# Mamba-2 block and mixture of experts on one core: late steps of a tile put in another order, another way into the experts, and five down products per experts' tile in place of six

## What is computed

```python
# block: y of the state-space layer, 1024 inner channels, 16 heads of 64, state 128
zxbcdt = u @ in_proj_w.T                    # z, xBC, dt
xBC = silu(conv_b + causal 4-tap conv of xBC)
y = Y_diag + Y_off + x * D_skip             # decays from cumsum(dt * A), states carried on
y = y * silu(z); y = y * rsqrt(mean(y*y) + EPS) * norm_w
o = y @ out_proj_w.T
# experts: 8 experts, hidden width F = 192, top 2 per token
gate, up = x @ w_gate_proj[e].T, x @ w_up_proj[e].T
out = sum_e weight[e] * ((silu(gate) * up) @ w_down_proj[e].T)
```

## Time and profile before

| what | us |
|---|---|
| median of 3 runs | 699.69 |
| the profiled execution | 697.2 |
| its span in the profile | 695.2 |
| TensorE busy | 637.0 (92%) |
| VectorE busy | 507.8 (73%) |
| ScalarE busy | 373.6 (54%) |
| GpSimd busy | 294.0 (42%) |
| DMA, mean over the span | 116 GB/s |

### The profile page before, as it was taken

One profiled execution on the slowest core, in us unless ns is written; L12 is line 12 of the kernel. 1 busy time (PEld: TensorE's weight loads), 2 busy tenths in 40 slices (PEclk: granted clock), 3 DMA queues, 4 the chain that ended last, 5 costly groups with the idle time before them and its releaser, 6 DMA issues.

```text
span 695.2 us, 12667 instructions
## 1 busy us (share of the span) xinstructions
PE 637.0 (92%) x4215; PEld 522.4 (75%) x4216; DVE 507.8 (73%) x1098; ACT 373.6 (54%) x787; POOL 294.0 (42%) x209
## 2 busy tenths in 40 slices
PE   4998899999999999989999989898988899999991
PEld 3896687868879678776877967665677788899981
DVE  6998868877977887787797698999786644444430
ACT  4778936564654754557376373638245444444431
POOL 2011344526435454453544424341136665656641
PEclk9999999999999999999999999998999999999996
DMA  8672014305113131530412304083594766767663
GB/s 269 231 288 92 1 39 145 122 11 173 60 64 122 62 123 32 151 123 1 152 51 103 96 28 130 1 272 115 172 305 80 132 123 117 125 120 123 125 100 45
DMA packets 31890, 80.38 MB, mean 116 GB/s; under 512 B 4768, under 2 KB 10016, under 8 KB 29664
## 3 DMA queue, kind: packets, MB, share of 16 engines
q1 hardware_dynamic: 22784, 58.23, 25.4%
q0 software_dynamic: 9056, 21.50, 17.1%
HBM read 59.93 MB, written 19.79 MB: 115 GB/s over the span
## 4 chain that ended last, share of the span: by engine, by line
PE 61%; DVE 17%; issue 7%; DMA 7%; ACT 5%; POOL 2%; SPq 0%; DVEq 0%; ACTq 0%; POOLq 0%
PE pi L1471 17%; PE po L1510 11%; PE pg L1685 9%; PE pd L1698 7%; DVE xs L959 5%; PE py L1566 3%; PE py L1573 3%; PE px L1668 2%; DMA out<-yo,idx 2%; DVE y L1244 2%; PE pxb L1557 2%; PE pxb L1588 2%; ACT m L675 1%; DMA m<-cs_d 1%; DMA out<-o 1%
## 5 line engine op out<-in xcount | busy, mean ns | idle before, releaser
L1471 PE MATMUL pi<-xh,whl 128*128 128x256 f32 x1152 | 165.1, 286 | 1.8 <-DVE zs L965 1.3
L1471 PEld LDWEIGHTS pi<-xh,whl 128*128 128x128 f32 x1152 | 146.3, 188 | 4.6 <-issue 2.4
L959 DVE SCALAR_TENSOR_TENSOR xs<-raw,conv_w,xs 128x256 f32<-128x256 f32 x240 | 112.1, 532 | 11.0 <-ACT xs L650 10.9
L1510 PE MATMUL po<-wo,y 128*128 128x512 f32 x256 | 114.8, 602 | 0.5 <-DVE y L1256 0.5
L1471 PE MATMUL pi<-xl,whl 128*128 128x256 f32 x576 | 91.7, 281 | 0.0
L1510 PEld LDWEIGHTS po<-wo,y 128*128 128x128 f32 x256 | 48.1, 193 | 55.4 <-issue 55.2
L551 POOL DMA_INDIRECT out<-yo,idx x39 | 62.0, 1590 | 61.2 <-ACT yo L817 32.4
L675 ACT ACTIVATE m<-m,cs_tok 128x128 f32<-128x128 f32 x256 | 79.7, 389 | 0.5
L1471 PEld LDWEIGHTS pi<-xl,whl 128*128 128x128 f32 x576 | 78.4, 188 | 0.0
L1685 PE MATMUL pg<-ew,xgh 128*128 x312 | 64.6, 349 | 0.0
L524 POOL TENSOR_TENSOR carry<-carry,cd 128x1024 f32<-128x1024 f32 x14 | 27.8, 1987 | 79.6 <-PE py L1566 79.6
(11 more groups left out here) (220 smaller groups left out, 1161.9 us busy)
## 6 DMA issues: line engine op xcount, KB each, us to landing
m<-cs_d SPq DMA_DIRECT2D x16, 1024.0 KB, 6.5
e<-cs_d SPq DMA_DIRECT2D x30, 256.0 KB, 4.6
ew<-in_w_gu SPq DMA_DIRECT2D x8, 768.0 KB, 9.5
w_as_read<-in_w_in SPq DMA_DIRECT2D x9, 512.0 KB, 8.3
res<-in_x SPq DMA_DIRECT2D x16, 256.0 KB, 2.8
out<-o SPq DMA_DIRECT2D x16, 256.0 KB, 2.0
xin<-in_x SPq DMA_DIRECT2D x6, 512.0 KB, 3.6
xn_d<-xin SPq DMA_DIRECT2D x6, 512.0 KB, 2.8
```

Of the source, the lines that this page charges most:

```text
L959: dve.scalar_tensor_tensor(out=xs[par][:, b, :], in0=raw[:, b, k:k + GT], scalar=conv_w[:, b, k:k + 1], in1=xs[par][:, b, :], op0=ALU.mult ...
L1471: mm = pe.matmul(bank[:, hf, :], whl[:, weight(g, n), lo, k, hf * P:(hf + 1) * P], xx[:, k, :], start=k3 == 0, stop=k3 == 11)
L1510: mm = pe.matmul(po[:, :], y[:, b, :], wo[:, b, :], start=b == 0, stop=b == XB - 1)
```

## The change

It does four things.

1. **Even tiles 2 to 12.** VectorE does `finish(t - 1)` after `own(1)` and `carried()`, no longer before them. SyncE's store of that output and load of the next residual go into the odd tile after, behind `load_decays2`.
2. **Tiles 13 to 15.** `probabilities` goes behind `carried()` in tile 13; `experts_of_tiles` goes to tile 15, in two parts (4 and 7 instructions). ScalarE's high halves of expert 0 go behind the `btok` copy of tile 15.
3. **The seam.** Two more buffers take the gathered rows of slot tiles 2 and 3, so these wait for the end of `own` in tile 15 and not for the turning of tiles 0 and 1. GpSimd waits for `factor(15)` before gathers 4 and 5, and then itself stores the last tile's output once `finish(15)` is done. SyncE no longer does.
4. **Five down products.** `h` is 256 channels wide: channels 0 to 127, then 128 to 191 twice (two instructions on VectorE). The down weights' second block holds channels 128 to 191 twice too, with the high half of the weights in partitions 0 to 63 and the low rest in 64 to 127. So one product gives high x (high + low) of the rest. The weights of an expert take 128 partitions where they took 96; `down_low` is two instructions.

```diff
-ph = [phs[0:FH, i, :, :] for i in range(2)]
+ph = [phs[:, i, :, :] for i in range(2)]
...
+xg_more = [Area(nc, second + i * D * 4, zs_at)(f"xg{2 + i}", [P, D]) for i in range(2)]
+hh = [es(f"hh{i}", [P, 2, P], F32R) for i in range(2)]
+hl = [es(f"hl{i}", [P, 2, P], F32R) for i in range(2)]
...
                 if t > 1 and c == 1:
                     load_decays2(t)
+                    if t < T - 2:
+                        store(t - 2)
+                        load_res(t - 1)
...
-                if t:
+                if t and (c == 1 or t == T - 2):
                     store(t - 1)
                     load_res(t)
...
-            store(T - 1)
-            sp.wait_ge(o_out, 16 * T)
+            sp.wait_ge(o_out, 16 * (T - 1))
...
             def gather(j):
-                if j >= 2:
+                to, arrived = (xg_more, xg_more_in) if j in (2, 3) else (xg, xg_in)
+                if j in (2, 3):
+                    pool.wait_ge(yd, 2 * T)
+                elif j in (4, 5):
+                    pool.wait_ge(gtr, j - 3 + CR)
+                elif j > 5:
                     pool.wait_ge(gtr, j - 1 + CR)
...
-            for j in range(4):
+            for j in range(6):
                 gather(j)
-            factor(T - 1)
+                if j == 3:
+                    factor(T - 1)
+            pool.wait_ge(o_done, T)
+            pool.dma_start(out_t[T - 1], o[:, :]).then_inc(last_out, 16)
             for j in range(1, J + 2):
-                if j + 3 < J:
+                if 2 < j < J - 3:
                     gather(j + 3)
...
-                    gate_up_high(act, 1)
-                    down_high(act, 1)
+                    for e in range(2):
+                        gate_up_high(act, e)
+                        down_high(act, e)
...
-            dve.tensor_tensor(d_lo(e), d_lo(e).bitcast(F32), d_hi(e).bitcast(F32), ALU.subtract).then_inc(d_lo_done, 1)
+            dve.tensor_tensor(d_lo(e)[:, 0:D], d_lo(e)[:, 0:D].bitcast(F32), d_hi(e)[:, 0:D].bitcast(F32), ALU.subtract)
+            dve.tensor_tensor(d_hi(e)[FR:P, D:2 * D], d_lo(e)[FR:P, D:2 * D].bitcast(F32),
+                              d_hi(e)[FR:P, D:2 * D].bitcast(F32), ALU.subtract).then_inc(d_lo_done, 1)
...
                 if t == T - 1:
+                    experts_of_tiles(0)
                     variance(t - 1)
                     decayed(0)
                     finish(t - 1)
+                    experts_of_tiles(1)
                     table()
...
-                if t == T - 3:
-                    probabilities()
...
-                if 0 < t < T - 1:
+                if 0 < t < T - 1 and (c == 1 or t == T - 2):
                     finish(t - 1)
...
                 if 0 < t < T - 2:
                     carried()
+                    if c == 0:
+                        finish(t - 1)
                 if t == T - 3:
-                    experts_of_tiles()
+                    probabilities()
...
-                dve.tensor_tensor(h[:, :], hg[:, :], pg[par][:, F:2 * F], ALU.mult).then_inc(h_done, 1)
+                dve.tensor_tensor(h[:, 0:F], hg[:, :], pg[par][:, F:2 * F], ALU.mult)
+                dve.tensor_tensor(h[:, F:2 * P], hg[:, P:F], pg[par][:, F + P:2 * F], ALU.mult).then_inc(h_done, 1)
...
-                for xx, ww in ((hh, dh), (hh, dl), (hl, dh)):
-                    for k in range(2):
-                        mm = pe.matmul(pd[par][:, :], xx[par][:, k, :], of(ww, e, k), start=n == 0, stop=n == 5)
-                        n += 1
+                pe.matmul(pd[par][:, :], hh[par][:, 0, :], of(dh, e, 0), start=True, stop=False)
+                pe.matmul(pd[par][:, :], hh[par][:, 0, :], of(dl, e, 0), start=False, stop=False)
+                pe.matmul(pd[par][:, :], hh[par][:, 1, :], of(dh, e, 1), start=False, stop=False)
+                pe.matmul(pd[par][:, :], hl[par][:, 0, :], of(dh, e, 0), start=False, stop=False)
+                pe.matmul(pd[par][:, :], hl[par][0:FR, 1, :], of(rest, e, 1), start=False, stop=True).then_inc(down, 1)
```

More of the change, by code:

```diff
@@ L28 @@
 E, F = 8, 192
-FH = F // 2
+FR = F - P
 T = TOKENS // P
@@ L1150, in table, with experts_of_tiles @@
                 dve.tensor_tensor(prob[:, :], prob[:, :], given(5), ALU.add).then_inc(prob_done, 1)
-            def experts_of_tiles():
+            def experts_of_tiles(part):
                 by_step = ef[:, :].rearrange("o (i two) -> o two i", two=2)
                 low, high = slice(0, (J - 3) // 2), slice(1, (J - 1) // 2)
-                dve.wait_ge(tab_in_s, 16)
                 route.after()
[L1157 to L1160, removed]
-                route.after()
-                route.step(dve.tensor_scalar(ef[:, 0:J], ef[:, 0:J], float(E - 1), None, ALU.min))
-                route.after()
-                dve.tensor_copy(eidx[:, :], ef[:, 0:J]).then_inc(eidx_done, 1)
+                if part == 0:
+                    route.step(dve.tensor_tensor(ecmp[:, :, :], tabc[0:1, TAB["tile"]].unsqueeze(2).broadcast_to([1, J, E]),
+                                                 end[0:1, :].unsqueeze(1).broadcast_to([1, J, E]), ALU.is_ge))
+                    route.after()
+                    route.step(dve.tensor_reduce(ef[:, 0:J], ecmp[:, :, :], AX.X, ALU.add))
+                    route.after()
+                    route.step(dve.tensor_scalar(ef[:, 0:J], ef[:, 0:J], float(E - 1), None, ALU.min))
+                    route.after()
+                    dve.tensor_copy(eidx[:, :], ef[:, 0:J]).then_inc(eidx_done, 1)
+                    return
+                route.step(dve.tensor_tensor(ecmp[:, 1:J, 0], ef[:, 1:J], ef[:, 0:J - 1], ALU.is_gt))
                 route.step(dve.scalar_tensor_tensor(out=pf[:, :], in0=by_step[:, 1, high], scalar=float(E),
@@ L1167, in experts_of_tiles @@
                 route.after()
+                route.step(dve.scalar_tensor_tensor(out=ecmp[:, 1:J, 1], in0=ecmp[:, 1:J, 0], scalar=16.0,
+                                                    in1=tabc[0:1, TAB["lag"]][:, 1:J], op0=ALU.mult, op1=ALU.add))
                 route.step(dve.scalar_tensor_tensor(out=pf[:, :], in0=pf[:, :], scalar=float(E),
@@ L1174, in experts_of_tiles @@
                 dve.tensor_copy(packed[:, :], pf[:, :]).then_inc(eidx_done, 1)
-                route.step(dve.tensor_tensor(ecmp[:, 1:J, 0], ef[:, 1:J], ef[:, 0:J - 1], ALU.is_gt))
-                route.after()
-                dve.wait_ge(ctap, 3 * CB * G)
-                route.step(dve.scalar_tensor_tensor(out=ecmp[:, 1:J, 1], in0=ecmp[:, 1:J, 0], scalar=16.0,
-                                                    in1=tabc[0:1, TAB["lag"]][:, 1:J], op0=ALU.mult, op1=ALU.add))
-                route.after()
-                dve.tensor_copy(landed[:, 1:J], ecmp[:, 1:J, 1]).then_inc(eidx_done, 1)
             statistics(0)
@@ L1663, in turn @@
             def turn(j, par, r):
-                pe.wait_ge(xg_in[par], r * 16 + 16)
+                rows = xg[par]
+                if static(j, 2, 3):
+                    pe.wait_ge(xg_more_in[par], 16)
+                    rows = xg_more[par]
+                elif static(j, 0, 1):
+                    pe.wait_ge(xg_in[par], 16)
+                else:
+                    pe.wait_ge(xg_in[par], r * 16)
                 if not static(j, 0):
@@ L1782 @@
     gu = np.concatenate([a["L0_ffn_w_gate_proj"], a["L0_ffn_w_up_proj"]], axis=1)
+    down = a["L0_ffn_w_down_proj"].transpose(0, 2, 1)
     arrays = {
```

34 lines of the change are left out of this document (15 added, 19 removed).

## The result

| | before | after |
|---|---|---|
| median, us | 699.41 (695.89 to 702.23, 10 runs) | 693.64 (689.95 to 694.61, 10 runs) |
| profiled execution, us | 697.2 | 692.66 |
| span, us | 695.2 | 690.9 |

The ratio is 0.9924 [0.9897, 0.9951]: faster by 5.8 us, where 15.4 were forecast. In the after kernel the lines are: turning of the next tile L1607, `carried` L1280, `off` L1585, `diag` L1592, projection L1529, turning of x L1694, gate and up L1711, the five down products L1721 to L1725, turning of h L1733, `h` in two pieces L1398 and L1399.

The account below looks back on a forecast made before the run. TensorE was taken to bound the kernel, nearly full in scan and experts. Terms 4.0 + 5.5 + 5.5 + 0.4 = 15.4 us took the profiled 697.2 to 681.8; plus 2.5 for the median, 684.3 us, range 678.5 to 691.5.

Parts of the forecast that it names:

- part 1: Even scan tiles: moving finish behind carried takes 0.66 us off each of six stalls, 4.0 us; ends 0 and 6.1.
- parts 2 and 3: Tiles 13 to 15 and first slot tiles: 2.6 + 4.1 - 1.2 for the clock, 5.5 us; ends 0 and 9.
- part 3: First slot tiles: timely gathers and an earlier store bring hidden tile 0 to 8 from 42.3 to 38.2, 4.1 us gained.
- part 4 with the tail: Experts: five down products save 0.19 us in each of 29 steps, 5.5 us, plus 0.4 behind the last gate product.
- The forecast's own sign of being wrong: Experts: a step of 4.1 us or more, where 3.98 us between down products was expected.
- The room in the loop through h: Experts: slack before TensorE must wait for h, put at 0.30 us in one tile and 0.39 in the next.
- the loop through h takes it all: Experts: second h instruction at full 0.23 us plus 0.15 more leaves five down products gaining 0; 690.2 us, chance 0.12.
- an h held up by GpSimd: Experts: second h instruction waits for GpSimd in each of 29 tiles; at 0.6 us longer, 707.2 us; chance 0.03.
- Part 2: Tiles 13 to 15: waits for own(0) and btok go; last projection starts 2.6 us sooner, before 1.2 off for the clock.
- the loss by the clock: Before the last projection: idle TensorE drops its clock, costing 1.5 to 2.7 us; with late gathers 689.8 us, chance 0.10.

Follow-up runs that it names:

- part 1 alone: Kernel before, with only finish moved behind carried in even tiles 2 to 12, with its store and residual load: 694.92 us, ratio 0.9932.
- parts 1 to 3: Changed kernel with the six down products of before, 96 channels each, and h in one instruction: 690.20 us, ratio 0.9877.
- parts 1 and 2: Kernel before with the moved finish and the new order in tiles 13 to 15, gathers and last store as before: 689.88 us, ratio 0.9892.
- the full product: Changed kernel with the fifth down product over all 128 rows, where it took 64: 688.99 us, ratio 0.9853.
- the order with the gate products first: Changed kernel, fifth product over 128 rows, gate products ahead of down products from slot tile 9: 692.28 us; with four gathered-row buffers too, 684.51 us.
- the three kernels with the extra products: Unread products added in tile 15: nine or four to the changed kernel with 128-row fifth product (690.62, 688.56 us); four with gate-first order, four buffers (683.24 us).

## Why the prediction was wrong

| term | forecast | measured, and from which kernels |
|---|---|---|
| part 1 | 4.0 | 3.9 (before, part 1 alone) |
| parts 2 and 3 | 5.5 | 4.7 (part 1 alone, parts 1 to 3) |
| of which part 3 | 4.1 | -0.3 (parts 1 and 2, parts 1 to 3) |
| part 4 with the tail | 5.9 | -3.4 (parts 1 to 3, after) |
| sum | 15.4 | 5.2 |

The terms are differences of medians from different rounds, so they add up to 5.2 and not to the 5.8 of the result. By the ratios to the kernel before in the same rounds, with intervals estimated from theirs, part 1 is 4.7 +- 1.6 us, parts 2 and 3 are 3.8 +- 3.1, part 3 is 1.0 +- 3.6 and part 4 is -3.3 +- 3.2. The sign of part 4 rests on the steps in the traces as well; the split between parts 2 and 3 is weak.

**Part 4 is the step that failed**, and in it the sentence "The fifth has 64 rows, but a product's time goes by its columns, which stay". The product itself is no slower, since the second of two neighbours takes 0.24 us; the two changes of rows cost 0.19 + 0.15 = 0.34 us a step, and 0.233 is what the sixth product had cost: +0.11, with 29 steps 3.1 us. The steps themselves took 2.5 us more than before (124.16 for 121.67). The forecast's own sign of being wrong, a step of 4.1 or more, is there. No row I showed of before had an operand of 64 rows between two of 128, so the cost needed bounds from both sides, and I gave it none. The Trainium skill has a rule that speaks to it and that I had not weighed: TensorEngine Tiling (Array Packing), Key Properties, says: "Changing tiling mode (not just tile) drains the TensorE". It stands under a list with modes of 32 and 64 rows. The slots of 0.42 and 0.43 us agree with it, but the skill gives no price, and nothing here asked for a mode, only for an operand of 64 rows; that the mode changed is not shown.

**The room in the loop through h** was the second mistake of the same part, hidden until the first was mended: with the full product the mean step is 4.194 for 4.196, a gain of nothing. So the rival "the loop through h takes it all" had the mechanism, at a chance of 0.12, and nearly the time: 690.2 us, against 688.99 with the full product. What I mis-sized is "When TensorE really waits for h, it is 0.26". That row is of an early tile, in which TensorE had been idle for 0.81 us. It is 0.29 again in slot tile 1 of the full-row kernel, but 0.45 and 0.55 in its steady steps, where TensorE is still busy with the down products when h comes; whether that is the reason is not shown. Against the 0.56 of the earlier trace rows that leaves 0 to 0.1 of room, not 0.30 to 0.39. The second h instruction then costs 0.48 - 0.35 = 0.13 (628.88 less 628.40, less one h), and taking it out gave 0.12 a step. That the loop is the bound is shown by the order with the gate products first: 3.93 us, 0.24 less than before, the 0.233 of the sixth product. With both bounds out of the way the medians go from 690.20 (parts 1 to 3) to 684.51, 5.7 us, near the 5.9 that I had for part 4 alone. The other rival of this part, an h held up by GpSimd, did not come: the second h instruction takes 0.21 us.

**Part 2 was probably undersized, and of its rival the loss by the clock came true.** The projection began 7.1 us sooner, against 6.6 forecast, and lost 1.43 by the clock, where I had 1.2. Alone, part 2 is worth 694.92 - 689.88 = 5.0 us by the medians and 2.8 by the ratios, where I had 2.6 - 1.2 = 1.4. The clock's cause, TensorE's idle time in tile 15, is shown: in the three kernels with the extra products the projection takes 7.1 us, in all the others with part 2 it takes 8.0 to 8.8. TensorE was ready for tile 15 sooner than I had shifted it (the projection in that tile begins 8.6 us sooner, 471.19 for 479.77, where I had 6.3), and VectorE, which I had bounding that tile, gave the start of the last one. That parts 2 and 3 together come near their 5.5 is luck, as far as the split can be trusted: one gave more than its term and the other nothing.

**Part 3** rested on rows 6: gathers late and the first add late. The gathers were hardly late any more: in these tiles the profile shows no wait of a product for rows, where it had four, 2.8 us. The add was, by 5.63 us: on GpSimd's queue the store is issued at 508.11, when `o` is ready, and the add can go only 6.2 us later. The wait for it had been 6.47 from SyncE's queue, so the new queue took little off. Of the 41.0 us, 1.6 are the slots of part 4 (39.4 with full rows) and 1.7 the store (37.7 without it), which leaves 37.7, near the 38.2 of the forecast. What remains are the waits for h, 6.9 us at the turning's weight loads with full rows, with the weights' rests on VectorE, which I had counted in. Why gathers on time gave so little is open. One sum in that part is off as well: 2.9 plus 3.1 is 6.0 and not 5.6, and the longest step in these tiles was 5.8.

**Part 1** was right in mechanism and size.

## What to carry to other kernels

Count a product by its columns only if its rows are of the same kind as its neighbours'; an operand filled up to 128 rows with something harmless was 4.7 us faster than one cut to 64. Before taking work from the engine that bounds a loop, work out the length of the loop that would bound it next, from rows in which the engine is as busy as it will be then, and the one after that: here the loop through h, and behind it the gathers, each hid the whole gain. Only with both out of the way did the step go from 4.17 to 3.93 us. Where a stall is moved, ask what the waiting engine then loses: its loads ahead, and its clock.

## What the runs showed of the hardware

- TensorE: from 128 rows to 64 or back costs 0.15 to 0.19 us each; from 128 to 96 nothing that a slot of 0.23 shows.
- A product 128x512 of this float32 kind is two instructions in the trace and takes 0.9 us at full clock (four in 3.61, eight in 7.03 to 7.13).
- With TensorE 15.53 of 20 us busy before and in the last projection the granted clock was 0.91 in that stretch (0.54 in 492:494, so 1.2 GHz for most of that), and the projection took 8.54 us; with 20.00 of 20 it was 1.00 and 7.13.
